# Folding b1 into the experts' W1 and making both parts of h straight from PSUM, in a two-layer gated transformer kernel

## The reference

```python
def _L0_ffn_ref(x, Wr, br, W1, b1, W2, b2):      # x is layer-normed; E = 8, H = 128, F = 512
    probs = jax.nn.softmax(x @ Wr + br, axis=-1)
    ...                                          # keep the largest until their sum reaches 0.8
    gate = probs * keep
    h = jax.nn.relu(jnp.einsum('bth,ehf->betf', x, W1) + b1[None, :, None, :])
    y = jnp.einsum('betf,efh->beth', h, W2) + b2[None, :, None, :]
    return jnp.einsum('bte,beth->bth', gate, y)
```

## Time and profile before

| | us |
|---|---|
| median of 3 runs | 219.61 (219.59 to 219.62) |
| span of the profiled execution | 218.5 |
| TensorE busy, 752 matmuls | 162.1 (74%) |
| VectorE busy | 177.2 (81%) |
| ScalarE busy | 97.9 (45%) |
| GpSimd busy | 82.2 (38%) |
| bytes moved | 12.85 MB, mean 59 GB/s |

### The profile page before, as it was taken

The page is one execution under the profiler, slowest core; times in us unless marked ns, Lnnn a source line. Parts: engine busy times, 40 slices in busy tenths (PEclk is TensorE's granted clock), DMA queues, the critical chain, the costliest instruction groups (busy, mean ns, idle before and its releaser), DMA issues.

```text
span 218.5 us, 2683 instructions
## 1 busy us (share of the span) xinstructions
PE 162.1 (74%) x752; PEld 122.0 (56%) x753; DVE 177.2 (81%) x353; ACT 97.9 (45%) x234; POOL 82.2 (38%) x83
## 2 busy tenths in 40 slices
PE   0889964999899798997989989899888592083012
PEld 0687853888676465665657657576545482040012
DVE  1957669587999999999999999997859996159724
ACT  2278334346383344624446244442279650054400
POOL 2500439130374282644826448269400631000010
PEclk9969965599999999999999999999999889558555
DMA  6970002300032401405014030110000000000003
GB/s 181 387 313 6 3 0 60 132 0 3 0 103 95 158 35 44 154 0 182 11 38 154 0 96 1 46 50 0 0 1 0 3 0 0 0 0 0 0 0 96
DMA packets 5354, 12.85 MB, mean 59 GB/s; under 512 B 600, under 2 KB 2776, under 8 KB 5088
## 3 DMA queue, kind: packets, MB, share of 16 engines
q1 hardware_dynamic: 4944, 12.53, 16.5%
q10 hardware_dynamic: 400, 0.20, 0.3%
HBM read 12.17 MB, written 0.56 MB: 58 GB/s over the span
## 4 chain that ended last, share of the span: by engine, by line
issue 26%; DVE 21%; POOL 19%; PE 18%; ACT 9%; POOLq 4%; DMA 2%; SPq 0%; DVEq 0%; ACTq 0%
PE ps L696 15%; POOL hlo L433 8%; DVE xn L1010 4%; POOL w1lo L386 4%; PE ps L693 4%; DVE hhi L1152 3%; POOL w2lo L391 3%; POOLq L67 3%; ACT PR L639 3%; POOL wqf L426 2%; DMA xs<-in_x 2%; DVE hmx L1307 2%; DVE l1w L1316 2%; ACT h L583 2%; DVE stats L999 1%
## 5 line engine op out<-in xcount | busy, mean ns | idle before, releaser
L583 ACT ACTIVATE h<-ps,b1cur 128x512 f32<-128x512 f32 x64 | 42.8, 688 | 51.6 <-DVE b1cur L1139 18.9
L433 POOL TENSOR_TENSOR hlo<-h,hhi 128x512 fp32r<-128x512 f32 x24 | 32.7, 1361 | 57.6 <-DVE hhi L1152 57.6
L1155 DVE TENSOR_TENSOR hlo<-h,hhi 128x512 fp32r<-128x512 f32 x40 | 46.1, 1152 | 1.4
L1152 DVE CAST hhi<-h 128x512 fp32r<-128x512 f32 x64 | 33.0, 533 | 2.4 <-ACT h L583 2.4
L696 PE MATMUL ps<-hhi,w2hi 128*128 128x512 f32 x64 | 27.6, 431 | 8.4 <-POOL hlo L433 7.5
L696 PE MATMUL ps<-xhi,w1hi 128*128 128x512 f32 x64 | 26.3, 411 | 2.0 <-POOL w1lo L386 2.0
L696 PE MATMUL ps<-xlo,w1hi 128*128 128x512 f32 x64 | 25.5, 398 | 0.0
L696 PE MATMUL ps<-xhi,w1lo 128*128 128x512 f32 x64 | 25.4, 397 | 0.0
L696 PE MATMUL ps<-hhi,w2lo 128*128 128x512 f32 x64 | 25.3, 395 | 0.0
L696 PE MATMUL ps<-hlo,w2hi 128*128 128x512 f32 x64 | 25.2, 394 | 0.0
L696 PEld LDWEIGHTS ps<-hhi,w2hi 128*128 128x128 f32 x64 | 12.0, 187 | 19.6 <-POOL hlo L433 13.4
(11 more groups left out here) (172 smaller groups left out, 302.8 us busy)
## 6 DMA issues: line engine op xcount, KB each, us to landing
raw<-in_experts SPq DMA_DIRECT2D x8, 512.0 KB, 4.8
G<-gates_dram SPq DMA_DIRECT2D x8, 512.0 KB, 4.0
l1w<-in_l1w SPq DMA_DIRECT2D x2, 1024.0 KB, 9.2
wf_raw<-in_ffnw SPq DMA_DIRECT2D x1, 560.0 KB, 11.6
xs<-in_x SPq DMA_DIRECT2D x2, 192.0 KB, 3.8
early_sb<-in_early SPq DMA_DIRECT2D x1, 333.0 KB, 3.7
out<-xs SPq DMA_DIRECT2D x2, 128.0 KB, 1.8
late_sb<-in_late SPq DMA_DIRECT2D x1, 223.0 KB, 4.0
```

Of the source, the lines that this page charges most:

```text
L433: eng.tensor_tensor(hlo[:, hs, :], h32[:, hs, :], hhi[:, hs, :].bitcast(F32), ALU.subtract).then_inc(s["lo_pool"], 1)
L583: eng.activation(h32[:, hs, :], ps[:, hs, :], ACT.Relu, bias=b1cur[:, slot, ft:ft + 1]).then_inc(s["h32_ready"], 1)
L1152: eng.tensor_copy(hhi[:, hs, :], h32[:, hs, :]).then_inc(s["hi_ready"], 1)
L1155: eng.tensor_tensor(hlo[:, hs, :], h32[:, hs, :], hhi[:, hs, :].bitcast(F32), ALU.subtract).then_inc(s["lo_dve"], 1)
```

## The change

- **b1 in W1.** The rows of a layer-normed x sum to zero over the features, so feature 0 is minus the sum of the others. The changed kernel puts 1 in the place of feature 0 (tile xm, normalised for features 1 to 127 only) and subtracts row 0 of W1 from rows 1 to 127; row 0 is replaced by b1. The product then holds b1. The router's weights and bias are treated in the same way (wr_sb, wr0, br).
- **Both parts from PSUM.** ScalarE writes hhi = relu(psum), VectorE hlo = max(psum, 0) - hhi in one scalar_tensor_tensor. h32, b1cur, the casts and GpSimd's share of hlo are gone.
- **Getting b1 in place.** TensorE transposes b1T, ScalarE copies it to b1rows (32 x 128), SyncE stores it to DRAM, waits, and loads 512 elements for each expert into partition 0 of raw. An expert's load becomes three DMAs: row 0 of W1 repeated into partitions 1 to 127 of w1r, rows 1 to 127 of W1, and W2. GpSimd's `fold` subtracts w1r from W1 before ScalarE copies the high part. fold(0) and fold(1) stand between the inv_rms steps.
- **Waits.** up(ft) waits for hlo(ft-2) by VectorE, where it waited for h32(ft-2) by ScalarE. hhi(ft) by ScalarE waits for down(ft-2).
- **Loops and ends.** All experts are written out. take_y of the expert before stands at parts 1 and 2, and the last y is added by VectorE alone.

```diff
+            def load_expert(e):
+                if e >= 2:
                     eng.wait_ge(s["w2_split"], e - 1)
-                eng.dma_start(raw[:, slot, :], experts[bass.ds(e, 1), :, :].rearrange("a p f -> p (a f)")).then_inc(
-                    s[f"raw_loaded{slot}"], 16)
+                    eng.wait_ge(s["w1_split"], e - 1)
+                loaded = s[f"raw_loaded{e % 2}"]
+                eng.dma_start(w1r[1:P, e % 2, :], experts[e, 0:1, 0:F].broadcast_to([P - 1, F])).then_inc(loaded, 16)
+                eng.dma_start(raw[1:P, e % 2, 0:F], experts[e, 1:P, 0:F]).then_inc(loaded, 16)
+                eng.dma_start(raw[:, e % 2, F:], experts[e, :, F:]).then_inc(loaded, 16)
+            def load_b1(e):
+                eng.dma_start(raw[0:1, e % 2, 0:F], b1_dram[FT * e:FT * (e + 1), :].rearrange("(a f) p -> a (f p)", a=1)).then_inc(
+                    s[f"b1_loaded{e % 2}"], 16)
...
+            eng.dma_start(wr0[:], late[0:1, late_w0:late_w0 + E].broadcast_to([P, E])).then_inc(s["wr0_loaded"], 16)
+            eng.wait_ge(s["b1_evac"], 1)
+            eng.dma_start(b1_dram, b1rows[:]).then_inc(s["b1_stored"], 16)
+            eng.wait_ge(s["b1_stored"], 16)
+            load_b1(0)
+            load_b1(1)
+            for e in (2, 3):
+                load_expert(e)
+                load_b1(e)
             eng.wait_ge(s["gt_evac"], 2)
             eng.dma_start(gates_dram, gateT[:]).then_inc(s["gt_stored"], 16)
             eng.wait_ge(s["gt_stored"], 16)
...
+            for e in range(2, E):
+                if e + 2 < E:
+                    load_expert(e + 2)
+                    load_b1(e + 2)
+                load_gates(e)
...
+            def fold(e):
+                eng.wait_ge(s[f"b1_loaded{e % 2}"], 16 * (e // 2 + 1))
+                eng.wait_ge(s[f"raw_loaded{e % 2}"], 48 * (e // 2 + 1))
+                w1 = raw[:, e % 2, 0:F]
+                eng.tensor_tensor(w1, w1, w1r[:, e % 2, :], ALU.subtract).then_inc(s["w1_folded"], 1)
...
+            eng.wait_ge(s["pool_const"], 1)
             inv_rms(0)
+            fold(0)
             inv_rms(1)
             inv_root(0, 4)
+            fold(1)
             inv_rms(2)
...
+            for e in range(2, E):
+                fold(e)
+                split_low(e)
...
-                        eng.activation(h32[:, hs, :], ps[:, hs, :], ACT.Relu,
-                                       bias=b1cur[:, slot, ft:ft + 1]).then_inc(s["h32_ready"], 1)
+                            eng.wait_ge(s["down_done"], nth(e0, f0, ci))
+                        eng.activation(hhi[:, hs, :], ps[:, hs, :], ACT.Relu).then_inc(s["hi_ready"], 1)
...
-                    eng.wait_ge(s["h32_ready"], 2 * (FT * e0 + f0 + 1))
                 for ci in range(2):
+                    if there:
+                        eng.wait_ge(s["lo_ready"], nth(e0, f0, ci))
...
-            def normalise(c, n):
+            def normalise(c, n, d0=0, dst=xn):
...
-                    last = eng.tensor_scalar(xn[:, j, :], xs[:, j, :], mv[:, j, 0:1], rstd[:, j:j + 1],
+                    last = eng.tensor_scalar(dst[:, j, d0:], xs[:, j, d0:], mv[:, j, 0:1], rstd[:, j:j + 1],
                                              ALU.subtract, ALU.mult)
...
+                        eng.wait_ge(s["hi_ready"], nth(e, ft, ci))
+                        eng.scalar_tensor_tensor(hlo[:, hs, :], ps[:, hs, :], 0.0, hhi[:, hs, :].bitcast(F32),
+                                                 ALU.max, ALU.subtract).then_inc(s["lo_ready"], 1)
+                    if e == 0:
                         router(ft)
+                    if (e, ft) == (1, 2):
+                        ffn_scales()
+                    if e == 1 and ft == FT - 1:
+                        take_y(0, 0)
+                        take_y(0, 1)
+                    if e >= 2 and ft in (1, 2):
+                        take_y(e - 1, ft - 1)
             for ci in range(2):
...
+                take_y(E - 1, ci)
```

More of the change, by code:

```diff
@@ L212, in build, with nth @@
             shi_ready hqf_ready hqf_ready_p hqb_ready dn_ready o_ready out_ready out_stored
-            raw_loaded0 raw_loaded1 g_loaded0 g_loaded1 whi_ready w1_split w2_split up_done h32_ready hi_ready
-            b1_ready lo_dve lo_pool down_done y_mul y_done y_added""".split()
+            raw_loaded0 raw_loaded1 b1_loaded0 b1_loaded1 wr0_loaded b1_evac b1_stored g_loaded0 g_loaded1 w1_folded whi_ready w1_split w2_split
+            wr_ready up_done hi_ready lo_ready down_done y_mul y_done""".split()
         s = {n: sem(n) for n in names}
         LAG = 2
[L220 to L227, removed]
+        def nth(e, ft, ci):
+            return 2 * (FT * e + ft) + ci + 1
         def h_slot(ft, ci):
@@ L238, in earlier @@
             m = ft - back
-            return e + m // FT, m % FT, not (isinstance(e, int) and FT * e + m < 0)
-        def fixed(e):
-            return isinstance(e, int)
+            return e + m // FT, m % FT, FT * e + m >= 0
         def tok(c):
@@ L332, in _ @@
             eng.wait_ge(s["gt_stored"], 16)
[L333 to L340, removed]
+            load_gates(0)
+            load_gates(1)
+            for e in range(2, E):
[3 more added lines that the diff above has]
+                load_gates(e)
             ov = out.rearrange("b (t p) d -> p b t d", p=P)
@@ L415, in _ @@
                               channel_multiplier=1).then_inc(s["mask_ready"], 1)
[L417 to L448, removed]
+            for e in range(2, E):
+                fold(e)
+                split_low(e)
+            eng.wait_ge(s["wmx_ready"], 1)
+            for c in range(7):
+                w = D if c < 6 else I
+                last = eng.tensor_scalar(wqf[:, c * D:c * D + w], wf_raw[:, c * D:c * D + w], winv[:, c:c + 1],
+                                         MAGIC, ALU.mult, ALU.add)
+            last.then_inc(s["wqf_ready"], 1)
             inv_root(0, 7)
@@ L516, in squares, with split_high @@
                 last.then_inc(s["sq_ready"], 1)
[L518 to L526, removed]
+            def split_high(e):
+                eng.wait_ge(s["w1_folded"], e + 1)
+                if e >= 2:
+                    eng.wait_ge(s["up_done"], nth(e - 2, FT - 1, 1))
+                eng.activation(w1hi[:, e % 2, :], raw[:, e % 2, 0:F], ACT.Copy).then_inc(s["whi_ready"], 1)
+                if e >= 2:
+                    eng.wait_ge(s["down_done"], nth(e - 2, FT - 1, 1))
+                eng.activation(w2hi[:, e % 2, :], raw[:, e % 2, F:], ACT.Copy).then_inc(s["whi_ready"], 1)
             def copy(dst, src, scale):
@@ L570, in _ @@
                 eng.activation(xT[:, t0:t0 + w], ps[:, X2B[c], 0:w], ACT.Copy).then_inc(s["xt2_evac"], 1)
-            def expert(e, slot):
-                eng.wait_ge(s["b1_ready"], e + 1)
+            for e in range(E):
                 for ft in range(FT):
@@ L596, in expert @@
                                 s["gt_evac"], 1)
[L597 to L606, removed]
+                    if ft == 2 and 1 <= e < E - 1:
+                        split_high(e + 1)
             for u, unit in enumerate(VWORK):
@@ L841, in down @@
                     mm(dst, wl, hhi[:, hs, :], False, ft == FT - 1).then_inc(s["down_done"], 1)
-            def expert(e, slot):
+            for e in range(E):
                 for ft in range(FT):
-                    up(e, ft, slot)
+                    up(e, ft)
                     e0, f0, there = earlier(e, ft, LAG)
                     if there:
-                        down(e0, f0, slot if ft >= LAG else 1 - slot)
-                    if fixed(e) and (e, ft) == (0, 1):
+                        down(e0, f0)
+                    if (e, ft) == (0, 1):
                         eng.wait_ge(s["pevac_d"], len(PREP) // 2)
+                        eng.wait_ge(s["wr_ready"], 1)
                         for t in range(NTILE):
-                            last = mm(ps[:, 7, t * E:(t + 1) * E], xT[:, t * P:(t + 1) * P], wr_sb)
+                            last = mm(ps[:, 7, t * E:(t + 1) * E], xT[:, t * P:(t + 1) * P], wr_sb[:])
                         last.then_inc(s["logit_ready"], 1)
-                    if fixed(e) and (e, ft) == (1, 1):
+                    if (e, ft) == (1, 1):
                         eng.wait_ge(s["gate_ready"], 1)
@@ L861, in expert @@
                                 last.then_inc(s["gt_ready"], 1)
-            expert(0, 0)
-            expert(1, 1)
-            with eng.Fori(2, E - 1, 2) as e:
-                for slot in range(2):
-                    expert(e + slot, slot)
-            down(E - 1, FT - 2, 1)
+            down(E - 1, FT - 2)
             vwork(0, 2)
-            down(E - 1, FT - 1, 1)
+            down(E - 1, FT - 1)
             vwork(2, 4)
             for half in range(2):
-                eng.wait_ge(s["y_done"], 2 * (E - 2) + half + 1)
+                eng.wait_ge(s["y_done"], 2 * (E - 1) + half + 1)
                 for j in range(4):
@@ L914, in _ @@
             last.then_inc(s["wgu_ready"], 1)
```

(25 more changed lines are left out.)

173 lines of the change are left out of this document (66 added, 107 removed).

## The result

The changed kernel takes 299.24 us (median of 4 runs, 297.83 to 301.62) against 219.6 us before: 1.363 times the time, 95% interval 1.355 to 1.371. The profiled execution took 297.83 us, of which 295.8 are the span.

The account below looks back on a forecast made before the run. The prediction took the lone DMA engine's queue as the bound: loads end at 213.0 us, up(7,0) at 217.5, last matmul at 235.6, 63.8 follow, span 299.4, plus 1.1: 300.5 us; range 284 to 325, nearly all of this case 276 to 332.

Parts of the forecast that it names:

- One engine for 127 rows: Expert loads: both 127-row DMAs run on one and the same DMA engine, whose queue becomes the bound; chance 0.83.
- 22 us per load, 1.4 for G: Lone engine's queue: 22 us for an expert's two 127-row DMAs and its W2 share, 1.4 us per G share.
- The start: Before the loop: b1 back at 59 us, second inv_rms at 60.3, 35.3 late, load of expert 2 issued at 71.1.
- The chain of loads: Loop: six loads in a row, 132 us, five G shares, 7, gates' store and wait, 1.9, ending at 213.0.
- TensorE after its idling: Last expert: the low clock after idling costs TensorE 2.0 us (0.7 to 2.2).
- The end: After the last down at 235.6 us: 63.8 us follow, span 299.4, and the median lies 1.1 above the span.
- The engines alone, 201.8 us: Whole kernel without the DMA queue: TensorE bounds at 11.1 us per expert, 219.6 - 16.8 - 1.0 = 201.8 us.
- rival 1: Expert loads: 127 rows dealt unevenly over 15 or 16 engines, so loads are hidden and 201.8 us result; chance 0.12.
- xm normalised in 127 elements: Before the loop: six operations stay held by GpSimd (0, the value taken) or run free, loop up to 2.7 us earlier.
- Rival 2: Expert loads: the two 127-row DMAs go to two different engines, 12.7 us an expert, 214 us; chance 0.03.
- Rival 3: Expert loop: slower three-operand hlo makes VectorE the bound again at 13.7 us per expert, 215 to 222 us; chance 0.02.
- The range: Within the one-engine case: eight loads -8 to +16, start +-3, clock and a later G +-4: 284 to 325 us.

Follow-up runs that it names:

- the cut at 112 against 113: Changed kernel with both 127-row DMAs split into 112 and 15 rows, 202.62 us, against the same split into 113 and 14 rows, 282.27 us.
- the split kernel: Changed kernel with both DMAs of 127 rows split into 112 and 15 rows: 202.62 us, 0.916 of the kernel before.
- the half dose: Changed kernel with only W1's rows 1 to 127 split into 112 and 15, the repeated row left whole: 223.08 us, 1.012 of the kernel before.

## Why the prediction was right, and where its terms were off

299.24 against 300.5 us: the mechanism held. Step by step:

- **One engine for 127 rows.** Shown, by the packets and by the cut at 112 against 113. That both DMAs take the same engine, inferred from two shapes, is shown too: the load's cost is the sum of the two, and two such DMAs at once took as long as two in a row. That it is the first of the 16 no run shows.
- **22 us per load, 1.4 for G.** The folds of experts 2 and 3 are 21.5 us apart with no G between them, forecast 22. The last three w1lo are 22.98 and 23.36 us apart with a G each, forecast 23.4. The rows alone cost 2 x 127 x 0.080 = 20.3. Between 191.5 and 211 us, in the last load, most slices of the DMA row show 25 GB/s.
- **The start.** b1 was folded at 57.77 (forecast 59) and the second inv_rms ran at 59.00 (60.3). The load of expert 2 was issued at 70.07 (71.1; by the sum's own shift it would be 36.06 + 35.3 = 71.4). That the second inv_rms and this issue stay 11.1 us apart was partly luck: the third inv_rms came 1.4 us sooner behind the second than before, and the first w1lo 1.3 us later behind the third, since it waited 1.31 us for ScalarE's w1hi.
- **The chain of loads.** From 70.07 to the last fold at 211.6 is 141.5 us; forecast 71.1 to 213.0, 141.9. Then up(7,0) came 3.8 us later, at 215.38 (4.5 forecast).
- **TensorE after its idling.** The clock was priced at 2.0 and cost 1.4:

```profile
215.38 0.79 PE L685 MATMUL ps<-xhi,w1hi 128*128 128x512 f32 x1 [9.39 <-POOL w1lo L406]
215.97 0.63 PE L685 MATMUL ps<-xlo,w1hi 128*128 128x512 f32 x1
216.40 0.63 PE L685 MATMUL ps<-xhi,w1lo 128*128 128x512 f32 x1
232.31 0.40 PE L685 MATMUL ps<-hhi,w2lo 128*128 128x512 f32 x1
```

  TensorE had stood idle for 9.39 us. From 215.3 to 217.0 us its granted clock is 0.50 (1.2 GHz) and the matmuls are 0.43 us apart, not 0.23; from 220 us on it is 1.00 (2.4 GHz). The first seven starts cover 3.01 us in place of 1.62. The last down ends at 232.7, 17.3 us after the first up; forecast 18.1.
- **The end.** 295.8 - 232.7 = 63.1 us, 63.8 forecast. Outside the span lie 2.0 us, not 1.1. The span came 3.6 lower than forecast (2.1 from up(7,0), 0.8 and 0.7 from the last two points), the rest 0.9 higher, and the profiled execution is 1.4 under the median: -3.6 + 0.9 + 1.4 = -1.3 us.
- **The engines alone, 201.8 us.** This was the sum for rival 1, and the split kernel is that case: 201.2 (199.6 to 202.7) on the same scale. hlo was taken as 0.74 and measured 0.687, the Relu as 0.69 ("reads a bias operand as before", but its row names none) and measured 0.596. The loop ran at TensorE's pace all the same, as argued. That TensorE bounds the engines is right: 11.23 us per expert, 48 x 0.2316 = 11.1 and 0.1.
- **xm normalised in 127 elements.** In the split kernel they are held as before (0.34 to 1.30 us), and the first up starts at 41.94 against 41.73: the value 0. In the changed kernel GpSimd's differences came later, all ran at 0.34, and the first up is 9.6 us behind the third inv_rms (62.00 to 71.60) and not 12.4. That is the upper value, 2.7. It paid nothing there, since the queue set the time.
- **Rival 2** put two engines at 214 us. Its sum doesn't hold together: 12.7 us an expert is more than TensorE's 11.3, so the queue would bind and not TensorE, and it misses the wait for the first G. No kernel had two engines; the half dose, the nearest, came to 222. In the changed kernel the same hole is larger and lies beside the queue's own work: TensorE waits 20.07 us for the hlo behind the first G. It costs nothing more, since expert 4's load was issued at 116.08, before TensorE resumed, and could be folded only at 142.25.
- **Rival 3** (a slow VectorE) has no support: hlo at 0.69 in every kernel.
- **The range.** Its terms add up to -15 and +23, that is 285.5 to 323.5, where the text has 284 to 325. Neither end was tried.

So of the 80 us lost, the engines' part gained 18 and the queue took 98 (299.2 - 201.2). The kernel with rows cut at 112 and 15 keeps the gain and beats the kernel before by 8.4% (7.7 to 9.1).

## What to carry to other kernels

Look at the partition count of every DMA before its bytes: 128, 112 or 126 rows used 16, 16 or 14 engines here, 127 or 113 rows one. If a row has to be left out, cut the rest at a multiple of 16, or send 128 rows and let the host put the odd one into the array. And ask what else is dealt a share on that engine: with the rows split, b1's trip cost nothing measurable and no engine waited for a G; behind a lone engine GpSimd waited 136.5 us for b1 and VectorE 60.9 us for G.

## What was not expected of the hardware

- SyncE itself is held while the lone engine works. The first DMA of a load, the repeated row, is issued in 0.23 to 0.80 us; it is the ones behind it that last: W1's rows up to 11.41 us, and W2, with its 128 good rows, 10.1 to 10.3 us each time. With the split rows every issue of a load took 0.3 to 1.0 us. That the engine's queue was full is inferred from these times.
- The Relu to a rounded (fp32r) output without a bias tile takes 0.596 us, where the one to f32 with its bias from a tile in SBUF took 0.688. Which of the two differences does it was not tried.
